# Scores of the first causal core contracted over 32 rows, one quarter of the matmul array for each head, two units issued together

## What is computed

```python
def _forward(x, wq, wk, wv, wo, fq1_w, ...):
    q, k, v = (proj(wq), proj(wk), proj(wv))                  # B, 16, L, 16
    q = (q @ fq1_w.T + fq1_b) * (q @ fq2_w.T + fq2_b)
    k = (k @ fk1_w.T + fk1_b) * (k @ fk2_w.T + fk2_b)
    scale = dk ** (-0.5)
    ...
    o = (inter + intra).reshape(B, H, L, dk)                  # = tril(q k^T) v * scale
    o = o * jax.lax.rsqrt(jnp.mean(o * o, axis=-1, keepdims=True) + EPS) * norm_w
    return o @ wo.T
```

## Time and profile before

| | us |
|---|---|
| median of 3 runs | 2063.25 (2061.75 to 2067.89) |
| the profiled execution | 2062.26 |
| its span | 2060.4 |
| PE busy | 1655.1 (80%) |
| DVE busy | 1342.0 (65%) |
| ACT busy | 1060.9 (51%) |
| POOL busy | 576.6 (28%) |
| mean granted clock of TensorE | 0.867 |
| the causal core: first mask on POOL to last copy on DVE | 54.03 to 119.66 |

### The profile page before, as it was taken

One profiled execution on the slowest core, in us unless ns is written; L12 is line 12 of the kernel. 1 busy time (PEld: TensorE's weight loads), 2 busy tenths in 40 slices (PEclk: granted clock), 3 DMA queues, 4 the chain that ended last, 5 costly groups with the idle time before them and its releaser, 6 DMA issues. The chain is left out here.

```text
span 2060.4 us, 28503 instructions
## 1 busy us (share of the span) xinstructions
PE 1655.1 (80%) x9533; PEld 1038.3 (50%) x9541; DVE 1342.0 (65%) x2664; ACT 1060.9 (51%) x2192; POOL 576.6 (28%) x466
## 2 busy tenths in 40 slices
PE   7957899999997879998489759875999777458924
PEld 3743566666775536655366447552222334216712
DVE  4767777676764448884577365346999647824467
ACT  2024556555543248894268348425999622515525
POOL 0406342322100018891121000003990000406710
PEclk9989999999999989999789869997555669778959
DMA  4000000000001001110000000007999600020000
GB/s 201 27 1 26 1 1 1 1 1 1 1 1 43 16 22 52 43 50 1 16 2 2 26 1 2 24 1 215 172 181 189 116 21 5 0 82 1 2 0 21
DMA packets 163008, 80.67 MB, mean 39 GB/s; under 512 B 155280, under 2 KB 156432, under 8 KB 161200
## 3 DMA queue, kind: packets, MB, share of 16 engines
q1 hardware_dynamic: 162720, 78.46, 15.9%
q10 hardware_dynamic: 144, 0.39, 0.0%
HBM read 39.44 MB, written 1.11 MB: 20 GB/s over the span
## 5 line engine op out<-in xcount | busy, mean ns | idle before, releaser
L1213 POOL TENSOR_TENSOR ss_u<-dx,b_rows 128x512 f32<-128x512 f32 x128 | 159.1, 1277 | 241.7 <-POOLq L181 225.7
L2034 ACT ACTIVATE qc_p<-qc_s,qc_bias,sq 128x1024 int16<-128x1024 f32 x128 | 154.2, 1204 | 16.5 <-DVE qc_bias L2000 6.4
L1295 DVE TENSOR_TENSOR_SCAN ss_h<-ss_decay,ss_u 128x512 f32<-128x512 f32 x128 | 146.5, 1204 | 24.2 <-PE ss_ht L1253 18.4
L932 ACT ACTIVATE gq_p<-gq_s,gq_bias,gq_rq 128x512 f32<-128x512 f32 x128 | 98.4, 773 | 119.2 <-DVE gq_bias L1002 119.2
L1998 DVE TENSOR_REDUCE qc_mx<-qc_s 128x1 f32<-128x1024 f32 x128 | 155.4, 1214 | 4.8 <-PE qc_s L1933 4.7
L865 POOL TENSOR_TENSOR gq_xw<-gq_x,weights 128x512 f32<-128x512 f32 x48 | 67.8, 1413 | 295.2 <-ACT gq_x L892 294.5
L1933 PE MATMUL qc_s<-kT,qT 64*128 64x512 bf16 x256 | 130.8, 617 | 15.0 <-ACT qc_p L2034 7.3
L1267 PE MATMUL ss_acc<-ss_hc,consts 128*128 128x512 f32 x256 | 130.8, 594 | 0.0
L800 PE MATMUL gq_s<-gq_KT,gq_QT 128*128 128x512 f32 x256 | 121.9, 599 | 3.6 <-ACT gq_p L932 3.6
L822 PE MATMUL gq_o<-gq_pT,gq_V 128*128 128x256 f32 x512 | 121.2, 379 | 1.4 <-DVE gq_pT L1036 1.4
L999 DVE TENSOR_REDUCE gq_mx<-gq_s 128x1 f32<-128x512 f32 x128 | 88.2, 691 | 43.9 <-PE gq_s L800 43.5
(11 more groups left out here) (579 smaller groups left out, 4121.9 us busy)
## 6 DMA issues: line engine op xcount, KB each, us to landing
b_rows<-b_rows SPq DMA_DIRECT2D x16, 512.0 KB, 3.7
weights<-in_weights SPq DMA_DIRECT2D x1, 6152.0 KB, 17.9
weights<-in_weights SPq DMA_DIRECT2D x1, 5248.0 KB, 16.7
weights<-in_weights SPq DMA_DIRECT2D x1, 3072.0 KB, 10.6
weights<-in_weights SPq DMA_DIRECT2D x1, 2156.0 KB, 7.4
qc_pT<-qc_p SPq DMA_TRANSPOSE x128, 3.3
weights<-in_weights SPq DMA_DIRECT2D x1, 1410.0 KB, 9.1
weights<-in_weights SPq DMA_DIRECT2D x1, 1282.0 KB, 6.3
```

What stands on the lines that cost most here:

```text
L932: nc.scalar.activation(pr[c % 2][:, t, :], sc[t][:, :], ACT.Exp, bias=bias[:, c, t:t + 1], scale=rq[b % 2][:, t, u:u + 1], accum_out=sm[:, ...
L1213: nc.gpsimd.tensor_tensor(u_in[i % 3][:, :], dx[:, m, hf * HT:hf * HT + HT], rows.rows[c % 2][:, n % rows.NEACH, :], ALU.mult).then_inc(in ...
L1295: nc.vector.tensor_tensor_scan(h[group % 2][:, m, :], decay[i % 2][:].rearrange("p b t -> p (b t)"), u_in[i % 3][:, :], 0.0, ALU.mult, ALU ...
L2034: nc.scalar.activation(pi[i % R][:, :], sc[i % 3][:, :], ACT.Exp, bias=bias[:, i:i + 1], scale=sq[:, t, h:h + 1], accum_out=sm[:, i:i + 1] ...
```

## The change

The first causal core gets a function of its own, `feature_core`; the second call keeps `causal_core`. Per unit, the scores are contracted over the 32 rows that hold the head and its neighbour, instead of 128: POOL makes two masked copies for each batch (even heads, odd heads) instead of eight. `tile_position` puts the matmul on the quarter of the array that these rows belong to, 32 rows x 128 columns. `head(u)` orders the units so that neighbours use different quarters. Two units are issued together, their parts interleaved, into four PSUM buffers instead of three. `outputs`, `out_turns`, ACT's copy, DVE's product and the lane sums are as they were, but for the order on PE.

```diff
+        parity=(p // 16 % 2 == np.arange(2)[None, :]).astype(f),
...
-        causal_core(g, q1, kT, heads(v), 16, heads(o), lanes=g.lanes)
+        feature_core(g, q1, kT, heads(v), heads(o), g.lanes)
...
+def feature_core(g, q, kT, v, o, lanes):
...
+    head = lambda u: 8 * (u % 16 // 8) + 2 * (u % 4) + u % 8 // 4
...
+        sc = [pb(f"fc_s{i}", [P, 384]) for i in range(4)]
...
+        qm = [sb(f"fc_qm{i}", [P, 2, 2, S]) for i in range(2)]
...
+            def _(pool):
+                for b in range(B):
+                    if b >= 2:
+                        pool.wait_ge(scored, 16 * (b - 1))
+                    for e in range(2):
+                        nc.gpsimd.tensor_scalar(qm[b % 2][:, e], q[:, :, b * S:b * S + S], g.parity[:, e:e + 1], 0.25,
+                                                ALU.mult, ALU.mult).then_inc(q_masked, 1)
+
+            def score_pair(u):
+                if u >= 4:
+                    nc.tensor.wait_ge(weighted, u - 2)
+                if u % 16 == 0:
+                    nc.tensor.wait_ge(q_masked, 2 * (u // 16) + 2)
+                for part in range(2):
+                    for x in (u, u + 1):
+                        b, h = x // 16, head(x)
+                        c, r, e, t0 = h // 8, h % 8 // 2, h % 2, b * S
+                        rows = slice(32 * r, 32 * r + 32)
+                        qh = qm[b % 2][rows, e, c, :]
+                        if part == 0:
+                            nc.tensor.matmul(sc[x % 4][:, 0:S], kT[rows, c, t0:t0 + P], qh, start=True, stop=True,
+                                             tile_position=(32 * r, 0))
+                        else:
+                            nc.tensor.matmul(sc[x % 4][:, S:S + P], kT[rows, c, t0 + P:t0 + S], qh[:, P:S], start=True,
+                                             stop=True, tile_position=(32 * r, 0)).then_inc(scored, 1)
...
+            def _(pe):
+                for i in range(0, U + 8, 2):
+                    if i == 56:
+                        lanes.turn(lane_summed, lane_turned)
+                    if i == 62:
+                        lanes.spread(lane_total, lane_turned)
+                    if i < U:
+                        score_pair(i)
+                    if i % 4 == 2 and 6 <= i < U + 4:
+                        outputs((i - 6) // 4)
+                    if i % 4 == 0 and i >= 8:
+                        out_turns((i - 8) // 4)
...
+                nc.vector.tensor_copy(o[:, 2 * b:2 * b + 2, h:h + 7:2, :], pot[:, :, :, 0:16]).then_inc(done, 1)
...
+                for u in range(U + 8):
...
+                    if u >= 8 and u % 4 == 3:
+                        finish((u - 8) // 4)
```

More of the change, by code:

```diff
@@ L3550, in _, with outputs, out_turns, finish @@
                 sp.wait_ge(v_out, 32)
+def feature_core(g, q, kT, v, o, lanes):
+    nc = g.nc
+    U = B * 16
+    G = U // 4
+    head = lambda u: 8 * (u % 16 // 8) + 2 * (u % 4) + u % 8 // 4
+    with ExitStack() as ctx:
+        sb, pb = places(g, ctx)
+        sc = [pb(f"fc_s{i}", [P, 384]) for i in range(4)]
+        po = [pb(f"fc_o{i}", [P, S]) for i in range(2)]
+        pot = pb("fc_ot", [P, 2, 4, 32])
+        qm = [sb(f"fc_qm{i}", [P, 2, 2, S]) for i in range(2)]
+        w = [sb(f"fc_w{i}", [P, 3, P]) for i in range(8)]
+        ob = [sb(f"fc_ob{i}", [P, S]) for i in range(2)]
+        lanes.scratch(ctx)
+        with stage(g, "fc_zeroed fc_q_masked fc_scored fc_weighted fc_used fc_out_stored fc_out_turned "
+                      "fc_done fc_lane_even fc_lane_odd fc_lane_summed fc_lane_turned fc_lane_chain fc_lane_total") as (
+                block, zeroed, q_masked, scored, weighted, used, out_stored, out_turned, done,
+                lane_even, lane_odd, lane_summed, lane_turned, lane_chain, lane_total):
+            @block.sync
+            def _(sp):
+                lanes.fetch((lane_even, lane_odd), lane_summed)
+            @block.gpsimd
+            def _(pool):
[22 more added lines that the diff above has]
+                                             stop=True, tile_position=(32 * r, 0)).then_inc(scored, 1)
+            def outputs(i):
+                b = i // 4
+                nc.tensor.wait_ge(weighted, 4 * i + 4)
+                if i == 0:
+                    nc.tensor.wait_ge(zeroed, 2)
+                if i >= 2:
+                    nc.tensor.wait_ge(out_stored, i - 1)
+                for k in range(4):
+                    nc.tensor.matmul(po[i % 2][32 * k:32 * k + 16, :], v[:, 2 * b, head(4 * i + k), :],
+                                     w[(4 * i + k) % 8][:, 0:2, :].rearrange("p a b -> p (a b)"), start=True, stop=False)
+                for k in range(4):
+                    last = nc.tensor.matmul(po[i % 2][32 * k:32 * k + 16, P:S], v[:, 2 * b + 1, head(4 * i + k), :],
+                                            w[(4 * i + k) % 8][:, 2, :], start=False, stop=True)
+                last.then_inc(used, 1)
+            def out_turns(i):
+                nc.tensor.wait_ge(out_stored, i + 1)
+                if i >= 1:
+                    nc.tensor.wait_ge(done, i)
+                for t in range(2):
+                    last = nc.tensor.transpose(pot[:, t].rearrange("p h d -> p (h d)"), ob[i % 2][:, t * P:t * P + P],
+                                               g.ident)
+                last.then_inc(out_turned, 1)
+            @block.tensor
+            def _(pe):
[10 more added lines that the diff above has]
+                        out_turns((i - 8) // 4)
+            @block.scalar
+            def _(act):
+                for i in range(G):
+                    act.wait_ge(used, i + 1)
+                    if i >= 2:
+                        act.wait_ge(out_turned, i - 1)
+                    nc.scalar.copy(ob[i % 2][:, :], po[i % 2][:, :]).then_inc(out_stored, 1)
+            def finish(i):
+                b, h = i // 4, head(4 * i)
+                nc.vector.wait_ge(out_turned, i + 1)
+                nc.vector.tensor_copy(o[:, 2 * b:2 * b + 2, h:h + 7:2, :], pot[:, :, :, 0:16]).then_inc(done, 1)
+            @block.vector
+            def _(dve):
+                for i in range(2):
+                    nc.vector.memset(po[i][:, :], 0.0).then_inc(zeroed, 1)
+                for u in range(U + 8):
+                    if u < U:
+                        dve.wait_ge(scored, u + 1)
+                        if u >= 8 and u % 4 == 0:
+                            dve.wait_ge(used, u // 4 - 1)
+                        nc.vector.tensor_tensor(w[u % 8][:], sc[u % 4][:, 0:384].rearrange("p (a b) -> p a b", a=3),
+                                                g.keep3, ALU.mult).then_inc(weighted, 1)
+                    if u >= 8 and u % 4 == 3:
+                        finish((u - 8) // 4)
+                    if u % 6 == 5 and u // 6 < lanes.CHUNKS:
+                        lanes.sum_chunk(u // 6, (lane_even, lane_odd), lane_summed)
+                    if u == 58:
+                        lanes.add_lanes(lane_turned, lane_chain, lane_total)
+                    if u == 66:
+                        lanes.keep(lane_turned, lane_total)
+                dve.wait_ge(done, G)
@@ L3571, in program @@
         g.eighth = const("eighth")
+        g.parity = const("parity")
         g.inv_freq = const("inv_freq")
```

## The result

The changed kernel takes 2087.72 us (median of 4 runs, 2086.73 to 2089.17), the kernel before 2065.57 us beside it (4 runs). The ratio is 1.0106 [1.0081, 1.0132]: slower by 1.1%, where 2082 (2057 to 2098) was forecast. The profiled execution of the changed kernel took 2086.93 us, with a span of 2085.1, against 2060.4 before.

The account below looks back on a forecast made before the run. PE bounds the stage, its clock staying at 0.50: 2.56 + 1.28 + 0.43 + 0.9 = 5.2 us a group, sixteen groups ending at 139.0 instead of 119.7, +19.3 us, so 2082 us (2057 to 2098).

Parts of the forecast that it names:

- What bounds the stage: First causal core: PE bounds it, DVE not far behind; a later stage end moves the whole program by as much.
- The start: Stage start: PE waits for two masks, not one, so first scores come at 55.5 us instead of 54.77.
- Pairs: Scores: two units run side by side on different quarters, 1.28 us a pair at 1.2 GHz, 0.64 at 2.4 GHz.
- The estimate from the Trainium skill: Scores: from 3.07 times for four 32-row strips, a pair takes 1.67 us and the kernel 2094.
- Changes of division: PE, each group: four switches of the array's division, 0.9 us in all at 1.2 GHz.
- The upper bound, serial weight loads: Changes of division: if a pair's two weight loads can't overlap, 0.85 us more a group, 2095 in all.
- The group and the stage: PE in the stage: 5.2 us a group at 1.2 GHz, stage end at 139.0 instead of 119.7.
- The clock: PE in the stage: with 0.58 of the rows in use over a group, the clock never rises from 0.50.
- the first rival: Stage: the clock rises anyway, DVE becomes the bound at 3.0 us a group, 2048 us; chance 0.16.
- the three stretches: Other stages, read as evidence that active rows raise the clock: 8-row and 64-row matmuls stay at 0.50, 128-row ones rise.
- Buffers and finish: PE in the stage: four PSUM buffers suffice, and at a slow PE the finish a turn waits for is always done.
- Behind the stage nothing should differ but by the shift.: Rest of the program after the first causal core: unchanged except for starting later; the forecast shift was +19.3 us.

Follow-up runs that it names:

- f2: e4 with the heads ordered so that a group's two pairs use the same two quarters of the array; 2082.82 us in one run.
- e5_same: The changed kernel with the heads in plain order, so both units of a pair lie on the same quarter; 2127.18 us in one run.
- e4: The changed kernel with the turn moved right behind the outputs, so a group's two pairs stand next to each other; 2057.56 us, ratio to before 0.9961.
- e1: The changed kernel with units contracting over 64 rows, four masks a batch, pairs on the array's two halves; 2056.82 us, ratio to before 0.9958.
- e2: The changed kernel with six added full-row matmuls near the stage's start, their output unread; median 2090.06 us.
- f1: e1 with e4's turn next to the outputs, and PE waiting for one mask at a time; 2056.59 us, ratio to before 0.9953.

## Why the prediction was right

**What bounds the stage.** Right: PE before, PE after. The 19.3 us by which the stage ends later went through to the end of the program. (One sum is loose: of the 3.81 us of a group before, 0.34 are left for the changes of division, not some 0.4; the 0.3 that the sum goes on with is right.)

**The start.** First scores were put at 55.5 and came at 55.74, because the first mask began 0.29 us later in this execution. The wait for a second mask costs what was said.

**Pairs.** Right: the two units start some 7 ns apart and take one unit's time. Forecast 1.28 us for a pair, found 1.59 with its change, of which 1.28 are the passes. In f2, where a pair follows a pair, its first half takes 0.85 us (88.17 to 89.02), which is one unit's at 1.2 GHz; e5_same shows what two units cost one after the other. The estimate from the Trainium skill ("TensorE: Matmul & The Clock Gate", Part 3), 1.67 us for a pair without changes, isn't borne out: with two tiles of 32 rows, two units took the time of one. No run here timed its case of four against one under its conditions, though e4's line of eight matmuls points the same way.

**Changes of division.** Forecast 0.9 us a group, found 0.93, by its parts 0.31 with a 128-column load behind it (forecast 0.26) and 0.13 into the outputs (0.12). The upper bound, serial weight loads, fell: one load of 0.16 is exposed, not two.

**The group and the stage.** Forecast 5.2 and an end at 139.0; found 5.20 and 138.93. That the end fits to 0.1 us is partly luck: the start came 0.24 us later, and from there to the end it took 83.2 us, not 83.5.

**The clock.** Right in its sign and for its reason: pairs of 64-row units, which fill the array's height together (e1), raise it; the same pairs with 32 rows each don't. The rule of the Trainium skill ("TensorE: Matmul & The Clock Gate", Part 1), by which a busy PE alone brings the clock back, led to the first rival; here PE was busy for all of 37.70 us at 0.50, and in f2 for all of 30.00. One of the three stretches that I read was less plain than I told it. Between the 64-row matmuls of the stage at 1450 us stand others of 128 rows (here from 1451.13 to 1451.54, some 0.4 us of every 1.38):

```profile
1451.13 0.38 PE L1943 MATMUL qc_o<-vi,qc_pT 128*128 128x16 f16 x8
```

So its "some 0.4" of the rows, whose working I didn't give, can't be held against this kernel's 0.58. The experiments carry the reason, not that stretch. And the step holds for this order only. I had reckoned with rows in use taken over the group, and took it that 32-row units in pairs keep the clock low however they are ordered; e4 shows that two pairs side by side add up to a full array, and then the 32-row kernel is 0.4% faster than the kernel before. What cost 1.1% is the turn between the two pairs, as much as the 32 rows. That the clock is back at 70.4 in e4 and not earlier or later, no run here explains.

**Buffers and finish.** At the low clock nothing waits, as said. At the full clock the turn waits for the finish (e1: 4.1 us), which the rival's 2048 left out. Its DVE bound of 3.0 us a group was right (e1: 3.2, with that wait), but it counted nothing for the rest of the program.

**"Behind the stage nothing should differ but by the shift."** This step failed. In the profiled executions the shift is 19.4 us where the next stage starts, 21.2 by the LayerNorm after the output projection, 23.7 at 660 us and 24.9 at 971; from there on it stays between 24.2 and 25.0, and is 24.7 at the end. The 5.4 us over the stage's 19.3 are the distance between the forecast for this execution (2081.6) and its time (2086.93). Stretches behind the stage in the changed kernel:

```profile
150.00:162.00 12.00, 6.99 (x24) 6.02 (x25) 5.31 (x16) 2.22 (x8) 0.00 (x0) 0.50 0.00 0
162.00:170.00 8.00, 5.44 (x25) 4.44 (x24) 6.02 (x21) 0.20 (x1) 0.00 (x0) 1.00 0.00 0
```

The low clock outlives its stage: it lasts until 162.0, which less the shift of 19.4 is 142.6. In the kernel before it also fell when the stage was over, but was back at 137.4, in this stretch:

```profile
136.00:140.00 4.00, 2.69 (x14) 2.38 (x13) 1.54 (x6) 1.39 (x5) 0.00 (x0) 0.82 0.00 0
```

That is the first 1.8 us. The other 3.5 lie where the clock's rises in later stages fell a little otherwise: a low stretch that lasts from 649.4 to 656.2 us before is twice as long with the change (670.6 to 684.2). They are hardly the change's: all eight other kernels of the table have a rest of 1999 to 2005.5 us, e1 and e4 too, whose clock was up when they left the stage, and the 1994.8 of the profile before is the odd one, an execution 4 us under the median of its 22 runs. Against that median the change adds 21.4 us, 2 more than the stage. Whether the 2 are the output projection alone, no run here parted.

## What to carry to other kernels

Before a contraction is cut to fewer rows to run several at once, count the rows at work at each moment, not the busy time: strips that run together count together, and a full-height instruction placed between two pairs keeps them apart. Look for that in the trace by the number of matmuls in a line and the granted clock of the stretch, and put the instructions that change the array's division next to each other. And once PE is faster than the engine behind it, more speed on PE gains nothing: all three good orders (e1, e4, f1) ended at DVE's 3.0 to 3.2 us a group, 0.4 to 0.5% under the kernel before.

## What the runs showed of the hardware that I had not expected

- Matmuls of two consecutive pairs on four different quarters of the rows run at once without being issued as one: four units took 1.02 us to their second half at 1.2 GHz (e4, 69.25 to 70.27), as two did (98.39 to 99.41).
- Weight loads of two quarters overlap: one exposed load of 0.16 us a pair at 1.2 GHz (changed kernel, 98.39 to 99.41).
- A risen clock can be lost in a busy stage: in e2 it fell at 68.1, after one wait of PE of 1.25 us and then a 32-row pair, and it didn't come back in the 70 us that were left of the stage. The same program once took 2055.57 and three times about 2090 us.
